# Wavelet mixing on one core: eight equal rounds of four pieces, batch innermost, first steps turned during the mixing

## The chip, the cores and the metric

One Trainium2 chip, one core in use. The metric is the device time of one execution in microseconds (us), the median over the runs of a kernel.

## The reference, cut to what matters

x is (8, 32, 512, 512) in float32: 8 batches of 32 channels, 256 images of 512 by 512. A wavelet transform of four levels is taken of every image, and only the coarsest coefficients (42 by 42 in each of four bands) are mixed between channels, by weights that differ from coefficient to coefficient; the rest passes through unchanged.

```python
yl, yh = _dwt2(x, _LEVEL)
yl_out = jnp.einsum('bixy,ioxy->boxy', yl, w_yl)
yh_out = yh[:-1] + [jnp.einsum('bicxy,iocxy->bocxy', yh[-1], w_yh)]
return _idwt2(yl_out, yh_out)
```

Since synthesis undoes analysis, the kernel computes out = x + synthesis(mixed coefficients - coefficients). The four bands of an image together are an 84 by 84 block of coefficients; the weights are 84 * 84 * 32 * 32 numbers, 28.9 MB, and each is used for the eight batches only.

## The kernel before, in words

The kernel has three phases, each written out per engine with its own semaphores; no planner sets the order. One image is 1 MB in float32.

**Analysis** (`turn1`, lines 373, 524 and 660): 32 turns of eight images. SP loads them into the eight slots of `x_sb`; PE reduces each along the height (`h_stage`, L333), ACT copies (L507), PE goes on along the width (L346, L357, L365) and the coefficients of 32 channels collect in `coef`. Once in a batch `channels_stage` (L378) turns them so that the channel and the row within a group of four lie on the partitions, and ACT's `copy_m` (L520) puts the result into `mix_sb`. The 84 rows are 21 groups ("lines") of four rows; four lines make a step, so that there are five full steps (FULL = 5) and a sixth with the one left-over line.

**Mixing** (`mix`, line 413): each full step is cut into six pieces of U = 14 columns (PARTS = 6), 30 pieces of 4 lines; the left-over line is another six pieces of one line each, at the end. For a piece, DVE (`build_low`, L680, three copies) and ACT (`build_high`, L553, one copy) lay the coefficients out block by block in one of two `diag` buffers; PE subtracts the old value (L420) and multiplies with the weights (L425, 56 matmuls, each recorded as two); ACT's `copy_mixed` (L560) copies the sum back to `mix_sb`. The weights come through a ring of three buffers (WBUFS = 3): SP waits for the piece that used a buffer (`weights_used`, L262) and loads 917,504 bytes (L258), or a quarter of that for a left-over piece. Two PSUM banks take turns. PE's loop `Fori(0, FULL)` has six pieces in its body; the left-over pieces are code of their own.

SP also loads six images of the next turn early (`load_early`, L265) into `work`: two ahead of the mixing, three among the pieces of the first step once the last channels are turned, one ahead of the left-over pieces.

**Synthesis** (`turn2`, lines 473 and 609): batches run backwards, the last one first. For each batch, `stage` takes its part of `mix_sb` (ACT's `copy_stage`, L585; for the first batch to be done DVE's L696, after all mixing), PE turns it back (`coefs_stage`, L449, four transposes a step), ACT's `copy_delta` (L593) stores it in `delta`. For each image ACT picks its block (L601), PE spreads it (`spread_stage`, L459), ACT copies (L607), PE finishes (`out_stage`, L469), DVE adds to the image (L703), SP stores it (L296), and POOL refills the slot (`refill`, L228) when the store has landed.

Within `mix_sb` an element is addressed as step, batch, line, column, so that the column is innermost:

```python
mix_sb = sb("mix_sb", [P, STEPS, BATCH, 4, ROWS])
```

Of the kernel before, what the change touches and what calls it, by code (L numbers as in the profile page):

```python
# [40 lines left out]
STEPS = -(-LINES // 4)  # L41
FULL = LINES // 4
U = 14
PARTS = ROWS // U
WBUFS = 3
QB = Q * BATCH
W_CHUNK = U * 4 * CHANNELS

# [76 lines left out]
def lines(v):  # L125
    return 4 if v < FULL else LINES - 4 * FULL


def wavelet_mix_kernel(nc, x, w_full, w_rest, consts, out):
# [3 lines left out]
    with ExitStack() as ctx:  # L133
# [6 lines left out]
        def sems(name, n):  # L140
# [6 lines left out]
        mix_sb = sb("mix_sb", [P, STEPS, BATCH, 4, ROWS])  # L147
        pick = sb("pick", [P, 2, ROWS])
        spread = sb("spread", [P, 2, SIZE])


        IMAGE = ROW_RUN * SIZE
        work = sb("work", [P, EARLY * IMAGE])
        along_h = work[:, 0:GROUP * SIZE].rearrange("p (m w) -> p m w", m=GROUP)
        at = GROUP * SIZE
# [3 lines left out]
        at += GROUP * ROWS  # L159
        coef = work[:, at:at + CHANNELS * ROWS].rearrange("p (r i) -> p r i", i=CHANNELS)  # L160
        used = at + CHANNELS * ROWS
        free = (EARLY * IMAGE - used) // IMAGE
        early = work[:, :].rearrange("p (a r w) -> p a r w", a=EARLY, r=ROW_RUN)
        early = [early[:, (e - free) % EARLY] for e in range(EARLY)]


        both = sb("both", [P, WBUFS * W_CHUNK + 2 * 4 * U * QB])
        w_sb = both[:, 0:WBUFS * W_CHUNK].rearrange("p (a n) -> p a n", a=WBUFS)
        at = WBUFS * W_CHUNK
        diag = both[:, at:at + 2 * 4 * U * QB].rearrange(  # L170
            "p (a l u n) -> p a l u n", a=2, l=4, u=U)
        delta = both[:, 0:2 * CHANNELS * ROWS].rearrange("p (a r) -> p a r", r=ROWS)
        assert 2 * CHANNELS * ROWS <= at
        stage = both[:, at:at + STEPS * Q * ROWS].rearrange("p (v r) -> p v r", v=STEPS)

# [4 lines left out]


# [16 lines left out]
        w_loaded = sems("w_loaded", WBUFS)  # L198
# [3 lines left out]
        mixed_copied = sems("mixed_copied", 2)  # L202
# [16 lines left out]
        def _(pool):  # L219
            nc.gpsimd.memset(mix_sb[:, FULL], 0.0).then_inc(cleared, 1)  # L220
# [22 lines left out]
        def _(sp):  # L243
# [12 lines left out]
            def load_w(c, v, weights):  # L256

                sp.dma_start(w_sb[:, c % WBUFS, 0:weights.shape[-1]], weights).then_inc(w_loaded[c % WBUFS], 16)  # L258

            def weights_used(c, v):  # L260

                sp.wait_ge(mixed[c % 2], PARTS // 2 * v + c // 2 + 2)  # L262
# [4 lines left out]
            for c in range(WBUFS):  # L267
                load_w(c, 0, w_full[c])
            for e in range(free):
                load_early(e)  # L270
            for c in range(WBUFS, PARTS):
                weights_used(c - WBUFS, 0)
                load_w(c, 0, w_full[c])
                sp.wait_ge(m_done, STEPS * BATCH)
                load_early(free + c - WBUFS)
            with sp.Fori(1, FULL) as v:
                for c in range(PARTS):
                    if c < WBUFS:
                        weights_used(c + PARTS - WBUFS, v - 1)
                    else:  # L280
                        weights_used(c - WBUFS, v)
                    load_w(c, v, w_full[PARTS * v + c])
            for e in range(free + WBUFS, EARLY):
                load_early(e)
            for c in range(PARTS):
                if c < WBUFS:
                    weights_used(c + PARTS - WBUFS, FULL - 1)
                else:
                    weights_used(c - WBUFS, FULL)
                load_w(c, FULL, w_rest[c])  # L290
# [24 lines left out]
        def _(pe):  # L315
            for a in range(2):
                pe.sem_inc(mixed[a], 1)
                pe.sem_inc(o_done[a], 1)
            pe.wait_ge(const_loaded, 16)
# [48 lines left out]
            def channels_stage(v, b):  # L368

                if v == 0:
                    pe.wait_ge(c_copied, CHANNELS // GROUP * (b + 1))
                if v >= 2:
                    pe.wait_ge(m_copied, STEPS * b + v - 1)
                for n in range(lines(v)):
                    h = Q * (4 * v + n)
                    last = nc.tensor.matmul(ps[:, 6 + v % 2, P * n:P * n + ROWS],  # L378
                                            coef[0:ROWS, h:h + Q].rearrange("p q i -> p (q i)"),
                                            const[0:ROWS, EYE:EYE + ROWS], start=True, stop=True, is_transpose=True)  # L380
                last.then_inc(m_done, 1)
# [25 lines left out]
            last_stage(HALVES * TURNS - 1)  # L407
            for v in range(STEPS):
                channels_stage(v, BATCH - 1)


            def mix(c, v, n):

                a, wb = c % 2, c % WBUFS
                w = w_sb[:, wb, 0:U * n * CHANNELS].rearrange("p (u l o) -> p u l o", u=U, l=n)
                pe.wait_ge(low_built[a], PARTS // 2 * v + c // 2 + 1)
                pe.wait_ge(high_built[a], PARTS // 2 * v + c // 2 + 1)
                pe.wait_ge(mixed_copied[a], PARTS // 2 * v + c // 2 + 1)
                for l in range(n):
                    nc.tensor.matmul(ps[32 * l:32 * l + 32, a, 0:U * QB], const[:, NEG:NEG + CHANNELS],  # L420
                                     diag[:, a, l].rearrange("p u n -> p (u n)"), start=True, stop=False)
                pe.wait_ge(w_loaded[wb], 16 * (PARTS // WBUFS * v + c // WBUFS + 1))
                for u in range(U):
                    for l in range(n):
                        last = nc.tensor.matmul(ps[32 * l:32 * l + 32, a, QB * u:QB * u + QB],  # L425
                                                w[:, u, l], diag[:, a, l, u], start=False, stop=u == U - 1)
                last.then_inc(mixed[a], 1)

            with pe.Fori(0, FULL) as v:
                for c in range(PARTS):  # L430
                    mix(c, v, 4)
            for c in range(PARTS):
                mix(c, FULL, lines(FULL))
            for a in range(2):
                pe.wait_ge(mixed_copied[a], STEPS * PARTS // 2 + 1)


            def coefs_stage(v, k, first=False):
# [3 lines left out]
                if first:  # L442
                    pe.wait_ge(first_staged, v + 1)
                else:
                    pe.wait_ge(staged, STEPS * (k - 1) + v + 1)
                if v >= 2:
                    pe.wait_ge(d_copied, STEPS * k + v - 1)
# [36 lines left out]
            for v in range(STEPS):  # L484
                coefs_stage(v, 0, first=True)
# [11 lines left out]
        def _(act):  # L497
            for a in range(2):
                act.sem_inc(mixed_copied[a], 1)
# [17 lines left out]
            def copy_m(v, b):  # L517
                n = lines(v)
                act.wait_ge(m_done, STEPS * b + v + 1)
                nc.scalar.copy(mix_sb[:, v, b, 0:n],  # L520
                               ps[:, 6 + v % 2, 0:P * n].rearrange("p (l r) -> p l r", l=n)[:, :, 0:ROWS],
# [20 lines left out]
            for v in range(STEPS):  # L542
                copy_m(v, BATCH - 1)


            def build_high(c, v, n):

                a = c % 2
                act.wait_ge(mixed[a], PARTS // 2 * v + c // 2 + 1)
                for q in range(Q - 1, Q):  # L550
                    part = slice(32 * q, 32 * q + 32)
                    src = mix_sb[part, v, :, 0:n, U * c:U * c + U].rearrange("p b l u -> p l u b")
                    last = nc.scalar.copy(diag[part, a, 0:n, :, BATCH * q:BATCH * (q + 1)], src)  # L553
                last.then_inc(high_built[a], 1)

            def copy_mixed(c, v, n):

                a = c % 2
                act.wait_ge(mixed[a], PARTS // 2 * v + c // 2 + 2)
                nc.scalar.copy(mix_sb[0:32 * n, v, :, :, U * c:U * c + U],  # L560
                               ps[0:32 * n, a, 0:U * QB].rearrange("p (u q b) -> p b q u", q=Q, b=BATCH),
                               ).then_inc(mixed_copied[a], 1)

            act.wait_ge(diag_cleared, 1)
            act.wait_ge(m_copied, STEPS * BATCH)
            build_high(0, 0, 4)
            build_high(1, 0, 4)
            with act.Fori(0, FULL - 1) as v:
                for c in range(PARTS):
                    copy_mixed(c, v, 4)  # L570
                    build_high((c + 2) % PARTS, v + (c + 2) // PARTS, 4)
            for c in range(PARTS):
                copy_mixed(c, FULL - 1, 4)
                after = FULL - 1 + (c + 2) // PARTS
                build_high((c + 2) % PARTS, after, lines(after))
# [166 lines left out]
```

## Time and profile before

| what | value |
|---|---|
| median of 3 runs | 2043.56 us (2043.24 to 2045.97) |
| the profiled execution's own time | 2043.87 us |
| its span in the profile | 2042.1 us |
| mean granted TensorE clock | 0.985 |
| analysis, up to the last matmul along the width | about 675 us |
| mixing, first to last matmul | 680.3 to 783.6 us |
| first `spread` matmul of the synthesis | 789.3 us |
| HBM traffic | 827 MB, mean 405 GB/s |

The profile's page shows one execution. Its parts give the busy time of each engine, forty slices of the span, the DMA queues, the chain of waits that ended last, and groups of instructions. PE is the matmul row and PEld the weight loads; SPq and POOLq are the queues' own DMA issues. "issue" is time in which an engine waited for nothing that the profile shows. Times in a timeline count from the start of the span.

### The profile page before, as it was taken

To read this page: it belongs to the slowest core of one execution; us is meant where nothing else is said; L and a number is where in the kernel's file an instruction comes from. 1 tells how busy PE (TensorE), PEld (TensorE's weight loads), DVE (VectorE), ACT (ScalarE), POOL (GpSimd) and SP (SyncE) were. 2 spreads that over 40 slices of the span, in tenths; PEclk is the share of its full clock that TensorE was granted. 3 is DMA by queue.
4 is the path that set the end of the run, shared out by engine and by line. 5 is a ranking of instruction groups with operands and counts; after the bars stand their busy time and mean duration, and the time that the engine had idled before them with its cause. 6 is when DMAs were issued, how large, how long until landed. Compare 5 with 4: busy or idle time off the path is not lost.

```text
span 2042.1 us, 44418 instructions
## 1 busy us (share of the span) xinstructions
PE 1882.5 (92%) x17580; PEld 943.2 (46%) x17580; DVE 827.2 (41%) x947; ACT 460.0 (23%) x1043; POOL 131.7 (6%) x249
## 2 busy tenths in 40 slices
PE   6999999999999778999999999999999999999996
PEld 3656666666666444444443343343333333334332
DVE  1222222222222354555544444444444444444443
ACT  1222222222222353121121121121121121112110
POOL 0000000000000000011111111111111111111110
PEclk8899999999999799999999999999999999999998
DMA  8999999999999695999999999999999999999998
GB/s 352 365 374 411 422 422 422 422 422 422 422 422 421 262 338 207 387 412 427 427 428 427 427 427 428 427 428 427 428 427 428 427 428 427 428 427 426 422 424 336
DMA packets 114794, 827.16 MB, mean 405 GB/s; under 512 B 12752, under 2 KB 13520, under 8 KB 17488
## 3 DMA queue, kind: packets, MB, share of 16 engines
q1 hardware_dynamic: 79920, 573.01, 67.8%
q0 software_dynamic: 34848, 253.77, 29.7%
q8 instruction: 21, 0.34, 0.1%
q14 instruction: 5, 0.04, 0.0%
HBM read 558.29 MB, written 268.44 MB: 405 GB/s over the span
## 4 chain that ended last, share of the span: by engine, by line
DMA 48%; PE 13%; issue 3%; DVE 2%; DVEq 0%; ACT 0%; POOLq 0%; SPq 0%
DMA out<-x_sb 32%; DMA x_sb<-x 14%; PE ps L469 8%; PE ps L459 2%; DMA both<-w_full 2%; DVE x_sb L703 2%; PE ps L425 1%; PE ps L420 1%; DMA both<-w_rest 0%; PE ps L449 0%; DVEq L715 0%; DVEq L133 0%; POOLq L228 0%; SPq L296 0%; ACT both L593 0%
## 5 line engine op out<-in xcount | busy, mean ns | idle before, releaser
L469 PE MATMUL ps<-spread,const 128*128 128x512 f32 x2048 | 940.0, 602 | 72.5 <-DVE x_sb L703 72.4
L703 DVE TENSOR_TENSOR x_sb<-ps,x_sb 128x1024 f32<-128x1024 f32 x500 | 592.7, 1220 | 626.1 <-DMA x_sb<-x 540.1
L469 PEld LDWEIGHTS ps<-spread,const 128*128 128x128 f32 x2048 | 373.5, 190 | 636.5 <-issue 407.8
L607 ACT COPY spread<-ps 84x512 f32<-84x512 f32 x256 | 148.8, 581 | 928.4 <-PE ps L459 928.0
L333 PE MATMUL ps<-x_sb,const 32*32 32x512 f32 x8192 | 293.9, 608 | 37.6 <-DMA x_sb<-x 31.6
L346 PEld LDWEIGHTS ps<-const,work 128*128 128x128 f32 x2048 | 252.0, 196 | 56.9 <-ACT work L507 42.3
L346 PE MATMUL ps<-const,work 128*128 128x84 f32 x2048 | 260.8, 281 | 3.4 <-ACT work L507 3.4
L459 PE MATMUL ps<-const,pick 128*84 128x512 f32 x512 | 261.3, 592 | 0.7 <-issue 0.7
L228 POOL DMA_DIRECT2D x_sb<-x x242 | 128.1, 529 | 1885.0 <-DMA out<-x_sb 1885.0
L507 ACT COPY work<-ps 128x512 f32<-128x512 f32 x256 | 131.4, 600 | 421.8 <-PE ps L333 421.8
L333 PEld LDWEIGHTS ps<-x_sb,const 32*32 32x32 f32 x8192 | 139.3, 104 | 141.5 <-issue 102.0
L652 DVE COPY work<-ps 128x336 f32<-128x336 f32 x256 | 129.9, 507 | 181.5 <-PE ps L346 181.5
L658 DVE COPY work<-ps 128x336 f32<-128x336 f32 x64 | 32.5, 507 | 325.9 <-PE ps L357 325.9
L459 PEld LDWEIGHTS ps<-const,pick 128*84 128x84 f32 x512 | 77.3, 153 | 121.5 <-issue 121.5
L680 DVE COPY both<-mix_sb 32x448 f32 (+1 forms) x108 | 52.9, 489 | 53.7 <-PE ps L425 50.0
L601 ACT COPY pick<-both 84x84 f32 (+1 forms) x256 | 66.8, 261 | 9.3 <-issue 9.3
L425 PE MATMUL ps<-both 128*32 128x32 f32 x3528 | 46.0, 206 | 24.7 <-DMA both<-w_full 12.7
L425 PEld LDWEIGHTS ps<-both 128*32 128x32 f32 x3528 | 43.8, 118 | 52.4 <-DMA both<-w_full 29.5
L357 PE MATMUL ps<-work,const 128*32 128x336 f32 x512 | 50.6, 468 | 0.6 <-DVE work L652 0.6
L365 PE MATMUL ps<-work,const 128*84 128x336 f32 x128 | 48.0, 458 | 0.6 <-DVE work L658 0.6
L420 PE MATMUL ps<-both,const 128*32 128x448 f32 x252 | 38.9, 623 | 2.8 <-ACT both L553 1.6
L593 ACT COPY both<-ps 84x512 f32 (+3 forms) x48 | 23.0, 529 | 65.5 <-PE ps L449 65.5
(23 smaller groups left out, 246.6 us busy)
## 6 DMA issues: line engine op xcount, KB each, us to landing
x_sb<-x SPq DMA_DIRECT2D x256, 1024.0 KB, 9.9
out<-x_sb SPq DMA_DIRECT2D x250, 1024.0 KB, 25.2
x_sb<-x POOLq DMA_DIRECT2D x242, 1024.0 KB, 11.0
both<-w_full SPq DMA_DIRECT2D x30, 896.0 KB, 6.7
work<-x SPq DMA_DIRECT2D x6, 1024.0 KB, 9.1
out<-work SPq DMA_DIRECT2D x6, 1024.0 KB, 10.1
both<-w_rest SPq DMA_DIRECT2D x6, 224.0 KB, 3.4
const<-consts SPq DMA_DIRECT2D x1, 888.0 KB, 4.5
```

Source lines behind the costliest of these rows:

```text
L228: pool.dma_start(x_sb[:, c], x_rows[first + c]).then_inc(x_reloaded[c], 16)
L333: last = nc.tensor.matmul(ps[to:to + TILE, m], const[part, A3H + TILE * r:A3H + TILE * r + TILE], x_sb[part, GROUP * a + m, r], start=r == ...
L346: last = nc.tensor.matmul(ps[:, 4 + m % 2, ROWS * k:ROWS * k + ROWS], along_h[:, m, P * k:P * k + P], const[:, A4 + ROWS * m:A4 + ROWS * ( ...
L420: nc.tensor.matmul(ps[32 * l:32 * l + 32, a, 0:U * QB], const[:, NEG:NEG + CHANNELS], diag[:, a, l].rearrange("p u n -> p (u n)"), start=T ...
L425: last = nc.tensor.matmul(ps[32 * l:32 * l + 32, a, QB * u:QB * u + QB], w[:, u, l], diag[:, a, l, u], start=False, stop=u == U - 1)
L459: nc.tensor.matmul(ps[0:ROWS, p], pick[:, p], const[:, SW:SW + SIZE], start=True, stop=True).then_inc(s_done[p], 1)
L469: last = nc.tensor.matmul(ps[:, 2 + k], const[:, SH + P * k:SH + P * k + P], spread[:, p], start=True, stop=True)
L507: nc.scalar.copy(along_h[:, m], ps[:, m]).then_inc(h_copied, 1)
L601: nc.scalar.copy(pick[0:ROWS, p], delta[0:ROWS, o]).then_inc(picked[p], 1)
L607: nc.scalar.copy(spread[0:ROWS, p], ps[0:ROWS, p]).then_inc(s_copied[p], 1)
L652: nc.vector.tensor_copy(turned[:, :, m], ps[:, 4 + m % 2, 0:SEGS * ROWS].rearrange("p (k r) -> p k r", k=SEGS),).then_inc(t_copied, 1)
L703: nc.vector.tensor_tensor(part, ps[:, 2 + 2 * half:4 + 2 * half], part, ALU.add).then_inc(added[half], 1)
```

## The change

- The left-over line is mixed first, in two pieces: its 84 columns are laid out as 4 times 14 and 4 times 7 columns in the places of the four lines. With the 30 full pieces that makes 32, run as eight rounds of four (PE `Fori(0, ROUNDS)`); the second piece's unused half is multiplied by zeros. Step 0 is now the one-line step.
- The weights have four buffers and the mixing four PSUM banks. All memory of mixing lies in `work`, apart from one early image that has a place of its own. SP loads four pieces and that image up front, two images when the last turn and the last coefficients are done, and the last three when the last four pieces are mixed.
- `mix_sb` has the batch innermost. `build_low` and `build_high` read runs of eight numbers, `copy_mixed` writes such runs, `copy_m` writes and `copy_stage` reads every eighth number.
- The last batch's channels are turned into six different PSUM banks, with no wait for copies between them; building of the first two pieces starts when step 0 is copied.
- In every round, between its second and third piece, PE makes the four transposes of `first_coefs`: those of a finished step in rounds 1, 2, 4, 5, 7 and after the last, and of no use in the other rounds. ACT's `copy_first` and `copy_delta` take the place of L696 and of the six turns after mixing.
- ACT's and DVE's mixing code is no longer a loop.

```diff
-        mix_sb = sb("mix_sb", [P, STEPS, BATCH, 4, ROWS])
+        mix_sb = sb("mix_sb", [P, STEPS, 4, ROWS, BATCH])
...
+LEFT = (U, U // 2)
+PIECES = len(LEFT) + PARTS * FULL
+RING = 4
+ROUNDS = PIECES // RING
+TURNED = {1: 0, 2: 1, 4: 2, 5: 3, 7: 4, 8: 5}
...
+            for k in range(RING):
+                load_w(k)
+            load_early(2)
+            sp.wait_ge(t_done, TURNS * SLOTS)
+            load_early(0)
+            sp.wait_ge(c_done, TURNS * HALVES)
+            load_early(1)
+            for k in range(RING, PIECES):
+                piece_mixed(k - RING)
+                load_w(k)
+            for e in range(3, EARLY):
+                piece_mixed(PIECES - RING + e - 3)
+                piece_mixed(PIECES - RING + e - 2)
                 load_early(e)
...
+            def mix(j, i):
+                a = j % 2
+                w = w_sb[:, j].rearrange("p (u l o) -> p u l o", u=U, l=4)
+                pe.wait_ge(low_built[a], RING // 2 * i + j // 2 + 1)
+                pe.wait_ge(high_built[a], RING // 2 * i + j // 2 + 1)
+                pe.wait_ge(mixed_copied, RING * i + j + 1)
+                if j >= 2:
+                    pe.wait_ge(m_copied, STEPS * BATCH)
...
+            def first_coefs(i):
+                pe.wait_ge(first_staged, i + 1)
+                pe.wait_ge(d_copied, i + 1)
+                for q in range(Q):
+                    last = nc.tensor.matmul(ps[0:ROWS, 6, P * q:P * q + P], first_stage[:, ROWS * q:ROWS * (q + 1)],
+                                            const[:, EYE:EYE + P], start=True, stop=True, is_transpose=True)
+                last.then_inc(d_done, 1)
+
+            with pe.Fori(0, ROUNDS) as i:
+                mix(0, i)
+                mix(1, i)
+                first_coefs(i)
+                mix(2, i)
+                mix(3, i)
+            first_coefs(ROUNDS)
...
-            for v in range(STEPS):
-                coefs_stage(v, 0, first=True)
...
+            for k in range(PIECES):
+                if k % RING == 0 and k // RING not in TURNED:
+                    act.sem_inc(first_staged, 1)
+                if k + 2 < PIECES:
+                    build_high(k + 2)
+                copy_mixed(k)
+                i, j = divmod(k, RING)
+                if j == 2:
+                    if i in TURNED:
+                        copy_delta(TURNED[i], 0, i + 1)
+                    else:
+                        act.wait_ge(d_done, i + 1)
+                        act.sem_inc(d_copied, 1)
+                for at, v in TURNED.items():
+                    if k == last_piece(v):
+                        copy_first(v, at)
...
-            for a in range(2):
-                dve.wait_ge(mixed_copied[a], STEPS * PARTS // 2 + 1)
-            for v in range(STEPS):
-                nc.vector.tensor_copy(stage[:, v], mix_sb[:, v, BATCH - 1].rearrange("p q r -> p (q r)"),
-                                      ).then_inc(first_staged, 1)
```

## Rows read from the trace of the kernel before

**Rows 1.** The page: span, 40 slices of DMA and GB/s, the synthesis's adds
```profile
span 2042.1 us, 44418 instructions
...
DMA  8999999999999695999999999999999999999998
GB/s 352 365 374 411 422 422 422 422 422 422 422 422 421 262 338 207 387 412 427 427 428 427 427 427 428 427 428 427 428 427 428 427 428 427 428 427 426 422 424 336
...
L703 DVE TENSOR_TENSOR x_sb<-ps,x_sb 128x1024 f32<-128x1024 f32 x500 | 592.7, 1220 | 626.1 <-DMA x_sb<-x 540.1
```

**Rows 2.** Windows: busy PE, PEld, DVE, ACT, POOL; PE clock, DMA share, GB/s
```profile
675.00:680.00 5.00, 2.71 (x23) 1.81 (x21) 2.73 (x6) 3.33 (x8) 0.00 (x0) 1.00 0.00 0
...
695.00:700.00 5.00, 2.99 (x118) 1.87 (x112) 1.59 (x3) 1.49 (x2) 0.00 (x0) 0.50 0.96 344
...
700.00:705.00 5.00, 2.20 (x99) 1.33 (x93) 0.86 (x3) 0.85 (x2) 0.00 (x0) 0.84 0.62 243
...
780.00:785.00 5.00, 3.85 (x74) 2.69 (x72) 1.45 (x6) 1.97 (x4) 0.00 (x0) 1.00 0.10 35
785.00:790.00 5.00, 3.70 (x26) 2.30 (x24) 0.84 (x4) 3.30 (x8) 0.00 (x0) 1.00 0.00 0
```

**Rows 3.** Waits from 670 to 800: us in total, times, longest
```profile
PE ps L425 <- DMA both<-w_full: 12.7, 15, 2.0
...
PE ps L425 <- issue: 10.7, 5, 4.3
```

**Rows 4.** Timeline of PE and of the DVE's first build, start and length in us
```profile
677.19 3.29 DVE L680 COPY both<-mix_sb 32x448 f32 x6 [2.61 <-ACT mix_sb L520]
...
680.27 1.72 PE L420 MATMUL ps<-both,const 128*32 128x448 f32 x8 [1.60 <-ACT both L553]
...
709.70 1.60 PE L425 MATMUL ps<-both 128*32 128x32 f32 x112
...
711.90 1.16 PE L425 MATMUL ps<-both 128*32 128x32 f32 x112
...
713.93 1.15 PE L425 MATMUL ps<-both 128*32 128x32 f32 x112
...
739.98 0.96 PE L420 MATMUL ps<-both,const 128*32 128x448 f32 x8 [0.32 <-issue]
...
771.27 1.16 PE L425 MATMUL ps<-both 128*32 128x32 f32 x112 [0.38 <-DMA both<-w_full]
```

**Rows 5.** DMA: 652 to 672, then 720 to 765; packets, MB, share; us to landing
```profile
q1 hardware_dynamic: 1204, 8.41, 101.4%
...
q1 hardware_dynamic: 2410, 15.33, 94.9%
...
both<-w_full SPq DMA_DIRECT2D x17, 896.0 KB, 6.7
```

**Rows 6.** The chain that ended last, from 766 on: start, length in us
```profile
766.59 7.72 DMA both<-w_rest
...
783.65 0.54 ACT mix_sb L560
...
785.41 0.59 ACT both L593
786.01 0.14 issue
786.14 0.62 PE ps L449 x4
...
789.30 1.92 PE ps L459 x4
```

**Rows 7.** Groups by form (first two: 664 to 800; last: from 800), mean ns
```profile
L553 ACT COPY both<-mix_sb 32x448 f32 x24 | 22.8, 950 | 0.6
L560 ACT COPY mix_sb<-ps 128x448 f32 x24 | 13.1, 544 | 39.8 <-PE ps L425 39.8
...
L585 ACT COPY both<-mix_sb 128x336 f32 x42 | 17.7, 471 | 0.0
```

More of the change, by code:

```diff
@@ L158, in wavelet_mix_kernel @@
         third = work[:, at:at + GROUP * ROWS]
[L159 to L168, printed above, removed]
@@ new lines, in wavelet_mix_kernel @@
+        w_sb = work[:, AT_W:AT_DIAG].rearrange("p (a n) -> p a n", a=RING)
+        diag = work[:, AT_DIAG:AT_DIAG + 2 * 4 * U * QB].rearrange("p (a l u n) -> p a l u n", a=2, l=4, u=U)
+        assert AT_DIAG + 2 * 4 * U * QB <= AT_EARLY
+        early = [0, IMAGE, AT_EARLY] + [AT_W + IMAGE * e for e in range(EARLY - 3)]
+        early = [work[:, e:e + IMAGE].rearrange("p (r w) -> p r w", r=ROW_RUN) for e in early]
+        APART = -(-(AT_W + IMAGE * (EARLY - 3) - 2 * IMAGE) // ROWS)
+        at = 2 * IMAGE + (APART + CHANNELS) * ROWS
@@ L316, in _ @@
             for a in range(2):
-                pe.sem_inc(mixed[a], 1)
                 pe.sem_inc(o_done[a], 1)
+            pe.sem_inc(d_copied, 1)
+            for c in range(RING):
+                pe.sem_inc(mixed_copied, 1)
             pe.wait_ge(const_loaded, 16)
@@ L408, in _ @@
             for v in range(STEPS):
[L409 to L420, printed above, removed]
+                channels_stage(v, BATCH - 1, LAST_BANKS[v])
@@ new lines, in mix @@
+            def mix(j, i):
[6 more added lines that the diff above has]
+                    pe.wait_ge(m_copied, STEPS * BATCH)
+                for l in range(4):
+                    nc.tensor.matmul(ps[32 * l:32 * l + 32, j, 0:U * QB], const[:, NEG:NEG + CHANNELS],
@@ L541, in _ @@
             copy_c(HALVES * TURNS - 1)
-            for v in range(STEPS):
[L543 to L554, printed above, removed]
@@ L567, in _, with build_high @@
[L567 to L575, printed above, removed]
-            for c in range(PARTS):
-                copy_mixed(c, FULL, lines(FULL))
-                if c + 2 < PARTS:
-                    build_high(c + 2, FULL, lines(FULL))
+            def build_high(k):
+                a, part = k % 2, slice(32 * (Q - 1), 32 * Q)
+                if k >= 2:
+                    act.wait_ge(mixed[a], k // 2)
+                nc.scalar.copy(diag_of(k)[part, :, :, BATCH * (Q - 1):BATCH * Q], lines_of(k)[part]).then_inc(high_built[a], 1)
@@ new lines, in copy_mixed, with copy_first @@
+            def copy_mixed(k):
+                act.wait_ge(mixed[k % 2], k // 2 + 1)
+                for to, of in sums_of(k):
+                    last = nc.scalar.copy(to, of)
+                last.then_inc(mixed_copied, 1)
+            def copy_first(v, i):
+                act.wait_ge(mixed_copied, RING + last_piece(v) + 1)
+                act.wait_ge(d_done, i)
+                nc.scalar.copy(first_stage[:].rearrange("p (q r) -> p q r", q=Q), mix_sb[:, v, :, :, BATCH - 1],
+                               ).then_inc(first_staged, 1)
@@ new lines, in copy_delta @@
+            def copy_delta(v, k, done):
+                n, h = lines(v), first_row(v)
+                bank = (6 + v % 2) if done is None else 6
+                act.wait_ge(d_done, STEPS * k + v + 1 + IDLE if done is None else done)
+                to = delta[0:ROWS, bass.ds(APART * (k & 1), CHANNELS), h:h + Q * n]
+                of = ps[0:ROWS, bank].rearrange("p (q l o) -> p o l q", q=Q, l=4)[:, :, 0:n]
+                nc.scalar.copy(to.rearrange("p o (l q) -> p o l q", q=Q), of).then_inc(d_copied, 1)
@@ L626, in turn2 @@
                         copy_stage(2 * c + 1, batch)
-            for v in range(STEPS):
-                copy_delta(v, 0)
-            act.wait_ge(d_copied, STEPS)
+            copy_delta(FULL, 0, ROUNDS + 1)
+            act.wait_ge(d_copied, STEPS + IDLE + 1)
             pick_image(0, 0)
```

203 lines of the change are left out of this document (99 added, 104 removed).

## The prediction

> **What bounds the kernel now.** I read the page's slices first. From the second slice on, the DMA engines are full, but in slices 13 to 16 (about 660 to 820 us) the rate falls from 422 to 262, 338, 207 and 387 GB/s [rows 1]. The synthesis runs at 427 GB/s, and DVE's adds there waited 540.1 us for images [rows 1]: the DMA is its bound, so an earlier first store should come out as an earlier end, one for one. The analysis is DMA-bound at 422 GB/s too, and the change leaves its loads alone. So the question is how much shorter the stretch without full traffic becomes, measured at the first `spread` matmul, now at 789.30 us [rows 6].
>
> The windows show three holes: from 675 to 680 nothing moves, from 700 to 705 the share is 0.62, and from 780 to 790 it is 0.10 and then 0.00 [rows 2]. The waits name what holds PE within the mixing: 10.7 us in five waits for "issue", in the middle of runs of L425 where no semaphore is waited for (I read these as PE waiting for its own code, on the first pass through the loop), and 12.7 us for weights [rows 3]. The timeline gives the pace: from the seventh piece's L425 (709.70) to the thirtieth's (771.27) are 23 pieces, 61.57 us, 2.68 us a piece [rows 4]. Pieces whose weights were there follow each other at 2.03 to 2.20 us (713.93 - 711.90 and 711.90 - 709.70) [rows 4]. A weight load takes 6.7 us from issue to landing [rows 5]; with three buffers that, the 1.16 us of L425 and some 0.2 us of semaphores make 8.06 us for three pieces, 2.69 us each. This agrees with the pace: the ring's latency sets it, not PE and not the DMA's full rate. That the DMA could do more is in the queue's rows: 8.41 MB in 20 us around 660, when weights were queued behind images, but 15.33 MB in 45 us (341 GB/s) in the mixing, at a share of 94.9% [rows 5]. I take the 94.9% as packets that lie half waiting, since the earlier window moved more at about the same share.
>
> **The change, part by part.**
>
> **Start.** PE's first L420 starts at 680.27, after DVE's six copies from 677.19 on and both `build_high` copies [rows 4]. Now only step 0, one line, need be copied before building; three copies take half of 3.29 us, 1.65 us. From some 676.8 on that gives a first matmul at 678.4: 1.9 us gained. PE has 21 transposes without waits meanwhile. The copies of step 0's piece back to `mix_sb` are four on ACT in place of one (4 * 0.54 = 2.2 us), but four PSUM banks are free before anyone needs them: nothing.
>
> **First round.** From 680.27 to 708.2 (L425 at 709.70 less its 1.5 us of L420) six pieces took 28 us, 4.7 us each, code waits and half clock included [rows 4]; the granted clock there was 0.50 to 0.84 [rows 2]. Four pieces cost 18.7 us by that, and four transposes 0.62 + 0.14 us [rows 6]: 19.5 us. Between bounds (all 10.7 * 4/6 = 7.1 us of code waits gone, or as before) I take 18 us: only weights are loaded beside the code now, while before an image came with each of three pieces; two images instead use the empty stretch from 675 on. End of round 0: 696.4.
>
> **Rounds 1 to 7.** PE needs 4 * 2.1 us, 0.76 us for the transposes and the 0.32 us that the loop's turn shows [rows 4]: 9.5 us. The DMA needs 4 * 0.9175 MB at 420 GB/s, 8.7 us. The ring of four gives a load 9.5 - 1.16 - 0.2 = 8.1 us to land, against 6.7 measured at a lighter rate. So PE sets the round: 7 * 9.5 = 66.5 us. PE was at half clock after the waits of the first pass (L425 1.60 us at 709.70, 1.16 later [rows 4]); I add 1.5 us for one or two such pieces. End of mixing: 764.4, against 783.65 [rows 6]. This includes the left-over line, which cost 17 us at the end before (766.59 to 783.65, 7.72 of it a wait behind an early image [rows 6]), and is now two pieces of 32.
>
> The transposes bring PE waits for `first_staged` and `d_copied`, with `mix` 2 and 3 queued behind them. In rounds 2 and 5 the step they need ended with the round before, so ACT has two pieces (4.2 us) for `copy_mixed`, `copy_first` and a build, together 0.54 + 0.5 to 0.8 + 0.95 us [rows 7]: hidden, with 2 us left. ACT waits for `d_done` ahead of `copy_first` in rounds 3 and 6, some 0.7 us, and builds a piece later by that; PE has a built piece in hand. Per piece ACT has 1.5 us of work and DVE 1.65 us [rows 4, 7], under the 2.1: nothing. Contiguous runs of eight should make the builds faster, at most by the 0.4 us between L553 and L560 [rows 7]; off the path.
>
> **Tail.** Before, 5.65 us lie between the last mixing matmul and `spread` (783.65 to 789.30 [rows 6]). Now it is one step: `copy_mixed` 0.54, `copy_first` 0.6, transposes 0.62, `copy_delta` 0.59, pick 0.26, five handovers of 0.1 or less: 3.2 us, if the code behind the loop is there. First spread at 767.6, 21.7 us earlier. SP's queue: the last three early images are issued as pieces 29 to 32 end, ahead of the first store. 3.1 MB at 422 GB/s are 7.5 us, and from the last piece's end to the first store lie some 3.2 + 6.8 us (before, 789.3 to 796.1). They fit in that hole.
>
> **Batch innermost.** ACT's `copy_stage` (42 times in the synthesis, 471 ns [rows 7]) now reads with a step of 32 bytes. The nearest row of a strided read is L553: 950 ns for 448 elements a partition, against 544 for L560 from PSUM [rows 7], 0.9 ns an element more. For 336 elements that is +0.3 us, 12.8 us in all, between nothing and that; and likewise for `copy_m`'s writes in the analysis, 35 full copies, at most 10.6 us. Both lie on ACT, beside a full DMA with loads in flight, so I cost them at nothing; without the cover at most 23 us would show. The Trainium skill ("SBUF — State Buffer", the note on cachelines) says that each access that leaves a 16-byte line pays, which takes in a step of eight fp32 numbers: by it the upper ends hold, and the sum would move only if ACT lay on the path. L680 on DVE, 0.55 us each with the same stride as L553 [rows 4], shows no such price on that engine.
>
> **Sum.** The steps are one chain of times, 678.4 + 18 + 66.5 + 1.5 + 3.2 = 767.6, and 789.3 - 767.6 = 21.7 us. 2043.87 (the profiled execution) - 21.7 = 2022.2 us; the median is 0.3 us lower, so **2022 us**.
>
> **The rivals.**
>
> **A. The DMA keeps its pace of 2.68 us a piece**, since its share was 94.9% already [rows 5]. For: that share. Against: 8.41 MB in 20 us. A round is then 10.7 us, 7 of them 8.5 us more: 2030.5 us. Chance 0.20.
>
> **B. The synthesis gives part back.** The three images at the end delay the first stores and refills, and strided copies hold up `spread` at seven batch boundaries: up to 7.5 us of images, up to 1 us a boundary. 2022 + 7 = 2029 to 2036 us. Against: the hole of 10 us, and ACT's idle share there. Chance 0.12.
>
> **C. The loop's code is fetched in every round.** Its waits took 10.7 us for six pieces [rows 3], 7.1 us for four; seven more rounds of that cost 50 us, so 2072 us, slower than before. It decides from 3.1 us a round on (21.7 / 7). For: the loop has transposes and four full pieces of code in it. Against: the old loop had six pieces, and its second pass shows 0.32 us at the turn and no wait inside a run [rows 4]. Chance 0.04. The Trainium skill ("Runtime: NRT & Kernel Launch", Instruction fetch mechanics) says that a taken branch whose target is outside a window of two pages forces a fetch, though it gives PE a larger memory than the others; by the two pages alone C would hold, and the old loop's second pass speaks against that.
>
> **D. Half clock through the mixing**: 3.2 us a piece (1.72 + 1.49, about the first one's) in place of 2.1 makes 31 us more, 2053 us. The clock fell when PE stood idle [rows 2], and there is less of that now. Chance 0.02.
>
> **How the numbers follow.** My forecast has 0.62. Its own range: code waits gone (-7), pieces at 2.03 us (-2), tail and start as said, 2013; up to the first round at 19.5 us and one code wait of 4.3 us behind the loop, 2028. With A and B the range is 2013 to 2034 us. A measurement of this kernel tells some 0.2%, 4 us, from no change. Faster by more than that: 0.93; within 0.2%: 0.02 (several costs of B in full, on top of A); slower: 0.05 (C, most of D).
>
> **What would show it.** Right: in the profile after, the first `spread` matmul near 768 us; 28 pieces after round 0 at 2.4 us each; the slices of GB/s without the 207; no copy of L696; PE's waits for weights under 5 us in all; synthesis of the same length as before, 1252.8 us from first spread to end (2042.1 - 789.3). Wrong: 10 us or more a round with PE waiting for weights (A); a synthesis over 1256 us (B); "issue" waits inside L425 runs after the first round (C); L425 runs of 1.5 us or more beyond 705 (D).

## The result and the profile after

The changed kernel takes 2006.43 us (median of 6 runs, 2001.11 to 2009.59) against 2040.74 us for the kernel before (6 runs, 2034.57 to 2045.97): a ratio of 0.983, with a 95% interval of 0.9809 to 0.9851. The gain is 1.7%, and the interval lies clear of 1. The forecast was faster, 2022 us with a range of 2013 to 2034; the measured time lies below the range. Two later pairs of the same kernels gave 0.9862 (0.9836 to 0.9888) and 0.9848 (0.9823 to 0.9873), so the gain is 27 to 34 us, where 21.7 were forecast. The three runs that I started from (median 2043.56 us) lie high among the runs of the kernel before: 23 later ones have a median of 2036.39 us.

The page of the changed kernel, profiled in its fastest run (2001.11 us; its span is 1999.5), shows the lines of [rows 1] again:

```profile
span 1999.5 us, 44393 instructions
...
PEclk9999999999999999999999999999999999999999
DMA  9999999999999898999999999999999999999997
GB/s 395 399 369 405 421 422 422 421 422 422 422 422 422 335 400 361 373 427 427 427 427 427 427 427 427 427 427 427 427 427 427 427 427 427 428 424 417 424 426 335
...
q8 instruction: 18, 0.29, 0.1%
...
L757 DVE TENSOR_TENSOR x_sb<-ps,x_sb 128x1024 f32<-128x1024 f32 x500 | 592.7, 1220 | 630.0 <-DMA x_sb<-x 543.0
```

The hole of four slices has become a dent: 335, 400, 361, 373 in place of 262, 338, 207, 387 GB/s. (A slice of the kernel before is 51 us, so its four run from 664 to 868 us; the prediction gave 820 us as their end, which changes nothing in its sum.) The adds of the synthesis wait for images as long as before (543.0 against 540.1 us), so the synthesis is still bound by the DMA.

The chain of waits of the changed kernel shows the new order (start, length in us). In this kernel L468 subtracts the old value, L473 multiplies with the weights, L482 transposes, L614 is `copy_first` and L512 the first `spread`:

```profile
669.79 0.96 PE ps L468 x8
...
672.94 0.95 issue
...
676.55 1.35 issue
...
680.20 1.18 issue
...
682.59 0.96 PE ps L468 x8
...
691.21 0.96 PE ps L468 x8
692.17 0.96 PE ps L473 x70
693.12 0.91 PE ps L468 x8
694.03 0.96 PE ps L473 x70
694.99 0.57 PE ps L482 x4
695.55 0.89 PE ps L468 x8
...
699.37 0.42 issue
699.79 0.96 PE ps L468 x8
...
742.83 0.54 ACT mix_sb L607
743.39 0.80 ACT const L614
744.24 0.64 PE ps L482 x4
744.87 1.01 issue
745.88 1.92 PE ps L512 x4
```

Round 0 runs from 669.79 to 682.59 (12.8 us) with three waits for issue, 3.5 us in all, against five and 10.7 us before [rows 3]. Then a round takes 8.58 us (691.21 to 699.79): four pieces of 1.90 us in the mean, 0.57 us of transposes, 0.42 us for the turn of the loop (the branch back to its start). The rounds that begin at 716.99 and 725.65 take 8.66 and 8.79 us. The tail from 742.83 to 745.88 is one step's copies and transposes, 3.05 us.

**Where the difference between the two profiles lies.** Executions differ in their analysis, so I count from the start of the last matmul along the width (L357 before, L400 after) to the first `spread` matmul. Before: 673.6 to 789.3, and 669.0 to 781.5 in a second trace, 115.7 and 112.5 us. After: 665.3 to 745.9, 670.3 to 752.7 and 665.1 to 745.7, that is 80.6, 82.4 and 80.6 us. The mean falls by 32.9 us (114.1 to 81.2). The synthesis, from the first `spread` to the end, took 1252.8 and 1253.0 us before and 1253.6, 1255.0 and 1255.1 us after: 1.7 us are given back there. The profiled pair differs by 42.6 us: 35.1 in this stretch and 8.3 because its analyses ended that far apart, less 0.8 in the synthesis.

### The profile page after: what moved, and what is told of

Read it like the earlier page. It is cut to its first block, busy times and chain, and to the rows that moved or that the text cites. A ratio compares the mean times of both kernels' runs of the same rounds, so it can differ in the third digit from the quotient of the medians.

```text
span 1999.5 us, 44393 instructions
## 1 busy us (share of the span) xinstructions
PE 1859.7 (93%) x17652; PEld 931.5 (47%) x17652; DVE 810.1 (41%) x930; ACT 480.8 (24%) x1047; POOL 132.2 (7%) x249
## 4 chain that ended last, share of the span: by engine, by line
DMA 58%; PE 33%; issue 4%; DVE 2%; SPq 1%; ACT 0%; DVEq 0%; POOLq 0%; ACTq 0%
DMA out<-x_sb 32%; DMA x_sb<-x 26%; PE ps L376 11%; PE ps L522 8%; PE ps L389 6%; PE ps L512 2%; DVE x_sb L757 2%; PE ps L473 2%; PE ps L468 1%; PE ps L400 1%; SPq L300 1%; PE ps L408 1%; PE ps L423 1%; ACT mix_sb L572 0%; PE ps L482 0%
## 5 line engine op out<-in xcount | busy, mean ns | idle before, releaser
L757 DVE TENSOR_TENSOR x_sb<-ps,x_sb 128x1024 f32<-128x1024 f32 x500 | 592.7, 1220 | 630.0 <-DMA x_sb<-x 543.0
L389 PEld LDWEIGHTS ps<-const,work 128*128 128x128 f32 x2048 | 246.5, 193 | 54.6 <-ACT work L557 40.2
L512 PE MATMUL ps<-const,pick 128*84 128x512 f32 x512 | 261.3, 592 | 1.0 <-issue 1.0
L389 PE MATMUL ps<-const,work 128*128 128x84 f32 x2048 | 255.4, 277 | 2.0 <-ACT work L557 2.0
L512 PEld LDWEIGHTS ps<-const,pick 128*84 128x84 f32 x512 | 77.3, 153 | 121.9 <-issue 121.9
L663 ACT COPY pick<-work 84x84 f32 (+1 forms) x256 | 66.7, 261 | 9.8 <-issue 9.6
L400 PE MATMUL ps<-work,const 128*32 128x336 f32 x512 | 50.5, 463 | 1.6 <-issue 1.0
L742 DVE COPY work<-mix_sb 32x448 f32<-32x448 f32 (+1 forms) x96 | 36.4, 380 | 36.9 <-PE ps L473 31.7
L473 PEld LDWEIGHTS ps<-work 128*32 128x32 f32 x3584 | 36.9, 109 | 20.4 <-issue 10.0
L473 PE MATMUL ps<-work 128*32 128x32 f32 x3584 | 37.5, 198 | 3.5 <-issue 3.5
L623 ACT COPY work<-ps 84x512 f32 (+3 forms) x48 | 24.0, 529 | 55.8 <-PE ps L502 54.5
L563 ACT COPY work<-ps 84x336 f32 (+1 forms) x64 | 27.8, 435 | 39.3 <-PE ps L408 39.3
```

The lines of the kernel that those rows point to most:

```text
L389: last = nc.tensor.matmul(ps[:, 4 + m % 2, ROWS * k:ROWS * k + ROWS], along_h[:, m, P * k:P * k + P], const[:, A4 + ROWS * m:A4 + ROWS * ( ...
L400: last = nc.tensor.matmul(ps[TILE * k:TILE * k + TILE, 6, 0:GROUP * ROWS], const[:, at:at + TILE], turned[:, k].rearrange("p m r -> p (m r ...
L473: last = nc.tensor.matmul(ps[32 * l:32 * l + 32, j, QB * u:QB * u + QB], w[:, u, l], diag[:, a, l, u], start=False, stop=u == U - 1)
L512: nc.tensor.matmul(ps[0:ROWS, p], pick[:, p], const[:, SW:SW + SIZE], start=True, stop=True).then_inc(s_done[p], 1)
L757: nc.vector.tensor_tensor(part, ps[:, 2 + 2 * half:4 + 2 * half], part, ALU.add).then_inc(added[half], 1)
```

## The experiments

Each starts from the changed kernel unless it says otherwise. "Rounds 1 to 7" is from the first L468 of round 1 to the start of the last L473; 60.0 us in the first profile (682.59 to 742.6), 61.6 in the second (687.85 to 749.4).

### Three and two weight buffers in use

```diff
-            for k in range(RING):
+            for k in range(3):
                 load_w(k)
...
-            for k in range(RING, PIECES):
-                piece_mixed(k - RING)
+            for k in range(3, PIECES):
+                piece_mixed(k - 3)
```

> The changed kernel, but SP loads the weights of piece k only when piece k-3 is mixed, so that only three of the four buffers are ever in use; the four PSUM banks stay. Theory (the fourth weight buffer sets the pace of the rounds): a load of some 7 us, 1.16 us of L473 and 0.2 us of semaphores per three pieces make 2.6 to 2.7 us a piece, rounds 1 to 7 grow from 60.2 us to 73 to 75 us, and the time from 2006 to about 2019 us. Rival (the round was short for other reasons, clock and faster builds): rounds of 8.6 to 9.0 us and a time within 3 us of the changed kernel.

With 2 in place of 3:

> The changed kernel, but SP loads the weights of piece k only when piece k-2 is mixed, so that two buffers are in use. Theory (a ring of n buffers gives a piece every (latency + 1.36 us) / n, until the DMA is full): the latency falls to 4.5 to 5.5 us with less in flight, so 3.0 to 3.4 us a piece, rounds 1 to 7 of 85 to 95 us, and about 2035 us. Rival (bytes set the pace): under 2.8 us a piece, under 2025 us.

Three: 2014.07 us (4 runs), ratio to before 0.9899 (0.986 to 0.9939). Two: 2031.82 us (10 runs), ratio 0.9967 (0.9949 to 0.9984). Rounds 1 to 7 take 70.7 us for three (685.27 to 756.0) and 82.3 us for two (693.99 to 776.3). The DMA view from 690 to 740 us has the latencies; first the changed kernel:

```profile
q1 hardware_dynamic: 3236, 20.62, 101.3%
...
work<-w_full SPq DMA_DIRECT2D x21, 896.0 KB, 7.3
```

Three buffers in use:

```profile
q1 hardware_dynamic: 2813, 17.90, 97.7%
...
work<-w_full SPq DMA_DIRECT2D x20, 896.0 KB, 6.5
```

Two:

```profile
q1 hardware_dynamic: 2379, 15.13, 87.3%
...
work<-w_full SPq DMA_DIRECT2D x17, 896.0 KB, 4.7
```

The last column is the median time to landing. With the 1.36 us of L473 and handovers, (4.7 + 1.36) / 2, (6.5 + 1.36) / 3 and (7.3 + 1.36) / 4 give 3.03, 2.62 and 2.17 us a piece; measured over 28 pieces are 2.94, 2.53 and 2.14. That the sums agree does not say what limits: with all buffers kept in use they must agree, since the latency of each is taken from the same run. What shows the cause is that the pace changed when the number of buffers alone did. So up to three buffers the ring's depth sets the pace, as the theory said; with four the latency has grown to 7.3 us and the DMA is at its full rate (20.62 MB in 50 us, 412 GB/s, at a share of 101.3%). A share of 97.7% still left 13% of the bytes on the table: the share is no proof of a full DMA. The fourth buffer is worth 70.7 - 60.0 = 10.7 us in the rounds here, a third of the 32.9 us. The expected ranges (73 to 75 us for three, 85 to 95 for two) began 2 to 3 us too high, and the times came out lower than expected too (2014.07 for 2019 us, 2031.82 for 2035 us).

### No transposes in the rounds

```diff
-TURNED = {1: 0, 2: 1, 4: 2, 5: 3, 7: 4, 8: 5}
+TURNED = {3: 0, 4: 1, 5: 2, 6: 3, 7: 4, 8: 5}
...
-                first_coefs(i)
                 mix(2, i)
                 mix(3, i)
-            first_coefs(ROUNDS)
+            for i in TURNED:
+                first_coefs(i)
```

with the three useless turns counted ahead, and ACT's copies after the last piece.

> The changed kernel with no transposes in the rounds; the six steps of the first batch are copied, turned and copied one after another when all is mixed, with a single stage buffer. Theory (rounds are at the DMA's full rate, 3.67 MB at 420 GB/s are 8.7 us): taking 0.6 us of PE out of each round leaves it at 8.5 to 8.7 us; the tail grows from 3.05 us to 6 * 2.1 = 12 to 13 us, and the time by 8 to 10 us. Rival (PE sets the round): rounds of 8.0 us, 4 us back in the rounds, and the time grows by 5 us only.

2018.94 us (4 runs), ratio 0.9915 (0.9883 to 0.9948): 10 to 14 us above the changed kernel's medians, where 8 to 10 were expected. Rounds 1 to 7 take 59.9 us (682.36 to 742.3), the same as with transposes: the theory holds. PE's weight loads wait for weights for 15.7 us now (second line), against 9.6 (changed kernel, first line):

```profile
PEld ps L473 <- DMA work<-w_full: 9.6, 22, 0.8
```

```profile
PEld ps L475 <- DMA work<-w_full: 15.7, 23, 0.8
```

So what the transposes took is waited for, and in the rounds PE (8.6 us with them) and the DMA (3.67 MB a round, 8.76 us at the 419 GB/s of its windows) are balanced within 2%: the changed kernel's rounds begin at PE's pace (8.58 and 8.60 us) and end at the DMA's (8.79). The tail grew from 3.1 to 14.7 us (742.3 to 757.0), 11.6 us where 9 to 10 were expected: PE fell to half clock in it, and four transposes took 1.09 us in place of 0.65. The windows show the clock (0.50) and the empty DMA (columns as in [rows 2]):

```profile
750.00:755.00 5.00, 2.25 (x9) 1.31 (x10) 0.00 (x0) 2.55 (x4) 0.00 (x0) 0.50 0.00 0
755.00:760.00 5.00, 3.99 (x8) 1.68 (x9) 0.00 (x0) 1.68 (x5) 0.00 (x0) 0.50 0.01 2
```

### PE's rounds written out

```diff
-            with pe.Fori(0, ROUNDS) as i:
+            for i in range(ROUNDS):
```

> The changed kernel with PE's eight rounds written out instead of a loop. Theory (the waits for issue inside runs of L473 in round 0 are PE waiting for its code, which the loop needs once): they appear in every round, some 3.5 us a round, in all 25 us, and more where the DMA is full; the time grows by 20 to 50 us. Rival (they are something else of the start, such as the clock or semaphores): waits in round 0 only, the time within 3 us, or 3 us less for the turn of the loop.

2052.49 us (6 runs), ratio 1.0077 (1.0052 to 1.0103): slower than the kernel before. Rounds 1 to 7 take 106.0 us. The page's instruction queue (packets, MB), the waits from 670 to 765 (us, times, longest) and PE's timeline of this kernel:

```profile
q8 instruction: 45, 0.74, 0.1%
```

```profile
PE ps L473 <- issue: 31.9, 21, 2.4
```

```profile
707.14 0.40 PE L473 MATMUL ps<-work 128*32 128x32 f32 x24 [1.85 <-issue]
...
711.17 0.38 PE L473 MATMUL ps<-work 128*32 128x32 f32 x21 [1.41 <-issue]
...
714.83 0.32 PE L473 MATMUL ps<-work 128*32 128x32 f32 x14 [1.56 <-issue]
...
719.20 0.27 PE L473 MATMUL ps<-work 128*32 128x32 f32 x7 [2.36 <-issue]
```

The instruction queue moved 45 packets of 16 KB in place of 18, 27 more for 28 more pieces of code, and there is one wait a piece in the rows above, each a little further on in the run of L473 (24, 21, 14 and 7 matmuls left). That is PE waiting for the next block of code. The waits in round 0 are the same thing, and the loop pays it once. The theory's price of 3.5 us a round was too low, though the total of 46 us lies in its range of 20 to 50: a written-out round costs 6.6 us more than one of the loop. The waits are 1.5 us each in the mean (31.9 in 21), 6.1 us for the four pieces of a round; in the first pass of the loop there were three waits, 3.5 us in all. PE also fell to half clock for some pieces (a granted clock of 0.66 from 720 to 730 us).

### The two images among the pieces of round 0

```diff
-            load_early(0)
             sp.wait_ge(c_done, TURNS * HALVES)
-            load_early(1)
             for k in range(RING, PIECES):
                 piece_mixed(k - RING)
                 load_w(k)
+                if k < RING + 2:
+                    load_early(k - RING)
```

> The changed kernel with the two images that it loads at the end of the analysis loaded behind the weights of the fifth and sixth piece instead, as the kernel before did. Theory (round 0 was shorter than forecast since PE's code came through an emptier DMA): the waits for issue in round 0 grow from 3.5 us to 6 to 9 us, PE falls to half clock for some pieces, round 0 grows from 12.8 to 16 to 20 us and the time by 3 to 7 us. Rival (the code comes at the same speed whatever the DMA carries): round 0 within 1 us, and only the 2 MB are paid later, up to 5 us where the rounds are DMA-bound, seen as weight waits in rounds 1 and 2.

2008.97 us (4 runs), ratio 0.9865 (0.9839 to 0.989), beside 2009.23 us and 0.9862 for the changed kernel run beside it: the 3 to 7 us that the theory gave do not show in the time. The trace has the effect on round 0 that it gave: the stretch from the last L400 (667.5) to the first `spread` (753.1) is 85.6 us, 4.4 more than the mean of 81.2. Round 0 took 16.6 us (671.98 to 688.62), with code waits of 0.41, 3.82 and 2.07 us, 6.3 in all, and the half clock behind them (L468 1.72 us instead of 0.96):

```profile
682.00 1.13 PE L473 MATMUL ps<-work 128*32 128x32 f32 x74 [3.82 <-issue]
682.98 1.72 PE L468 MATMUL ps<-work,const 128*32 128x448 f32 x8
...
687.40 0.79 PE L473 MATMUL ps<-work 128*32 128x32 f32 x68 [2.07 <-issue]
```

So the code does come more slowly while images are being moved. From the last L400 to the end of the span this kernel took 1338.9 us (667.5 to 2006.4), the changed kernel 1334.2, 1337.4 and 1335.7 in its three traces: 3.1 us more than their mean. Medians of four runs that spread over 4 to 6 us don't separate that from nothing.

### The same two images after the mixing

```diff
             load_early(2)
-            sp.wait_ge(t_done, TURNS * SLOTS)
-            load_early(0)
-            sp.wait_ge(c_done, TURNS * HALVES)
-            load_early(1)
...
                 load_early(e)
+            for e in range(2):
+                load_early(e)
```

> The changed kernel with the two images that it loads at the end of the analysis loaded behind the three late ones instead, as pieces end and before the first stores. Theory (an emptier DMA brings PE's code sooner, and the stretch between the last piece and the first stores has room for 2 MB more, 5 us): the waits for issue in round 0 fall from 3.5 us to 0.5 to 2 us, the synthesis keeps its 1253 to 1255 us, and the kernel is 1 to 3 us faster than the changed one. Rival (that stretch is already used up by the three images): the first stores land later, the synthesis grows by 3 to 5 us, and the kernel is 1 to 3 us slower.

> The changed kernel once more, beside the one with both images late, for a time on the same chip. Both theories: from the last matmul along the width to the first spread matmul 80 to 83 us, and its median within 4 us of 2007 us.

2008.85 us (6 runs) against 2005.12 us (5 runs) for the changed kernel beside it, with ratios to before of 0.9864 and 0.9848 whose intervals overlap: no gain shown, and a loss of 1 to 3 us (the rival) not excluded. PE's waits for code in round 0 stayed as they were (us, times, longest; L471 is this kernel's L473):

```profile
PE ps L471 <- issue: 3.5, 3, 1.6
```

So moving these two images out of the analysis's end did not shorten them. They do depend on what else is being moved, though: in round 0 they come to 2.2 us with two weight buffers in use (0.95, 0.68 and 0.62), 3.2 us with three, 3.5 us with four and 6.3 us with the images among the pieces. (With two buffers PE also waited 0.5 us for weights there, during which code could come.) The synthesis did not grow either, 1254.9 us, so the stretch between the last piece and the first stores takes the 2 MB; but nothing is won by it: from the last width matmul (668.6) to the end (2004.2) are 1335.6 us, where the changed kernel has a mean of 1335.8. The changed kernel's third trace came out as expected (80.6 us, 2005.12 us).

### The old layout alone

```diff
-        mix_sb = sb("mix_sb", [P, STEPS, 4, ROWS, BATCH])
+        mix_sb = sb("mix_sb", [P, STEPS, BATCH, 4, ROWS])[:].rearrange("p s b l r -> p s l r b")
```

> The changed kernel with the column innermost in the mixed coefficients again, as before. Theory (the new layout moves costs off and on ACT and DVE without touching the path): the builds go back to about 540 ns on DVE and 950 ns on ACT, the copies into the mixed coefficients from 844 to about 440 ns, and those to the stage from some 830 to about 470 ns; three DVE builds take 1.65 us against a piece of 1.9 us, so a round stays at 8.6 to 8.8 us and the time within 3 us. Rival 1 (the builds were what held PE before): rounds of 9 us and more, 3 to 8 us slower. Rival 2 (the dear copies at the seven batch boundaries cost the analysis something): the analysis ends 1 to 4 us earlier and the kernel is faster by that.

2011.25 us (4 runs), ratio 0.9874 (0.9836 to 0.9911); rounds 1 to 7 take 60.2 us (686.60 to 746.8). The forms in the mixing of this kernel (busy us, mean ns):

```profile
L742 DVE COPY work<-mix_sb 32x448 f32<-32x448 f32 x93 | 50.2, 540 | 23.0 <-PE ps L473 20.0 <-ACT mix_sb L572 2.1
...
L601 ACT COPY work<-mix_sb 32x448 f32<-32x448 f32 x31 | 29.3, 945 | 3.8 <-PE ps L473 2.8
L607 ACT COPY mix_sb<-ps 128x448 f32<-128x448 f32 x30 | 28.5, 950 | 1.8 <-PE ps L473 1.1
```

and of the changed kernel, in the mixing, the analysis and the synthesis:

```profile
L742 DVE COPY work<-mix_sb 32x448 f32<-32x448 f32 x93 | 35.6, 383 | 36.8 <-PE ps L473 31.7 <-ACT mix_sb L572 4.3
...
L601 ACT COPY work<-mix_sb 32x448 f32<-32x448 f32 x31 | 17.4, 561 | 25.1 <-PE ps L473 24.9
```

```profile
L572 ACT COPY mix_sb<-ps 128x336 f32 x35 | 24.7, 785 | 3.6 <-PE ps L423 2.9
```

```profile
L654 ACT COPY work<-mix_sb 128x336 f32 x42 | 31.5, 800 | 0.0
```

The layout moves costs in both directions and the rounds don't notice. With the old one ACT was busy 9.54 us of the 10 from 700 to 710, against 5.74 with the new one, but the DMA set the pace in both. (`copy_mixed` costs 950 ns here and not the 544 of [rows 7]; this version goes through the batches innermost, where the kernel before wrote runs of columns, so it is the old layout but not the old copy.) The dear copies at the batch boundaries cost the analysis nothing that its spread would show (669.0 us at a clock of 0.95 in the first 200 us).

### Both kernels once more

> The kernel before, once more, for a second trace of it. The two profiled executions differ by 8.3 us already in the analysis, which the change hardly touches. Theory (the start of an execution varies from run to run with the clock that PE has in its first 200 us): this trace's analysis ends anywhere from 665 to 675 us, with a granted clock below 1 in the first 200 us in proportion, and its mixing lasts 110 us as before (first to last mixing matmul 103 us). Rival (the change shortens the analysis): 673 us again, within 1 us.

> The changed kernel once more. Theory: from the last matmul along the width to the first spread matmul 81 us within 1 us, from there to the end 1253 to 1254 us, and an analysis that varies between executions by some us with the clock in the first 200 us. Rival (the analysis is shorter by the change): 665 us again, within 1 us.

2037.89 us (12 runs) and 2009.23 us (4 runs). The analysis ends anywhere between 664.9 and 677.0 us over the twelve traces of all versions (start of the last matmul along the width), and the clock of the first 200 us goes with it. The window of those 200 us in the kernel before (673.6 us), in the one with two buffers (677.0 us) and in the changed kernel (665.3 us); the last three columns are clock, DMA share and GB/s:

```profile
0.00:200.00 200.00, 173.16 (x2859) 112.08 (x2859) 43.12 (x80) 42.87 (x86) 3.61 (x7) 0.93 0.92 374
```

```profile
0.00:200.00 200.00, 173.82 (x2763) 111.25 (x2764) 43.97 (x81) 44.48 (x86) 3.61 (x7) 0.91 0.91 367
```

```profile
0.00:200.00 200.00, 172.30 (x2965) 112.74 (x2976) 46.48 (x86) 50.80 (x97) 3.61 (x7) 0.98 0.96 392
```

The second trace of the kernel before has 0.96 and 669.0 us, that of the changed kernel 0.97 and 670.3. So the spread of executions is there in both kernels, as the theory said. That the clock is its cause is not shown: the DMA's rate in these windows falls with it, and either could come first. With two traces of the kernel before, a small effect of the change on the analysis is not excluded.

For the rest the expectations were a little off: the mixing of the kernel before, first to last matmul, took 99 us in this trace in place of 103, and the changed kernel's second trace has 82.4 us for the stretch and 1255.0 us for the synthesis, where 80 to 82 and 1253 to 1254 were expected.

## Why the prediction was wrong in its size

The order of things was right: the synthesis stayed DMA-bound and moved forward with the first `spread`, the holes were where it said, the tail came out at 3.05 us (3.2 forecast), and the start, from the last width matmul to the first mixing matmul, at 4.5 us where 6.7 less 1.9, 4.8, were forecast. Two terms were too large, and the base was too high.

- **First round: 18 us forecast, 12.8 measured** (13.1 in the second trace). I scaled the old first round to four pieces, half clock included, and took 1.5 us off for the lighter DMA. But the code waits are 3.5 us and not some 5.6 (7.1 less 1.5), and in the first profile PE never fell to half clock in it. The experiment with the images in round 0 brings back 3.8 us of this (16.6 us) by the two steps named; the rest I can only argue: the old round carried three images, not two, and began at half clock (L420 1.72 us [rows 4]). My low bound for it, with the 7.1 us gone, was 12.4 us, so the measured 12.8 lies inside it. (The range took 7 us off the 18, which gives 11 and counts 1.4 us twice.)
- **Rounds 1 to 7: 66.5 + 1.5 us forecast, 60.2 measured** (682.59 to 742.83). This is the step that failed. The 2.03 us between pieces whose weights seemed to be there [rows 4] were read as PE's own pace, and PE was given 2.1 us a piece, 8.4 a round; measured are 1.90 and 7.6, with 0.57 us of transposes for 0.76 and 0.42 us at the turn for 0.32, which together make 8.58 for 9.48. The half clock for which 1.5 us were added did not occur in the first profile; the second trace has it at the start of round 1 and takes 61.6 us. The old interval of 2.03 us had waits in it. The weight loads of that piece in the kernel before:

```profile
713.16 0.16 PEld L420 LDWEIGHTS ps<-both,const 128*32 128x32 f32 x8 [0.21 <-DVE both L680]
...
713.59 0.13 PEld L425 LDWEIGHTS ps<-both 128*32 128x32 f32 x4 [0.28 <-DMA both<-w_full]
```

The second trace of the kernel before has two pieces without such waits, 1.76 us apart:

```profile
704.88 1.16 PE L425 MATMUL ps<-both 128*32 128x32 f32 x112
...
706.64 1.16 PE L425 MATMUL ps<-both 128*32 128x32 f32 x112
```

That error lies in the forecast's lower bound too ("pieces at 2.03 us, -2"), which is one reason why the range stopped at 2013. With PE's true pace the DMA's 8.7 us a round, which I had worked out and set aside, is as high: 8.6 us were measured, with and without the transposes. So "PE sets the round" failed as well: PE and the DMA set it together.

Together these are 5.2 + 7.8 = 13.0 us, against a stretch that ended 13.4 us sooner than forecast (80.6 us instead of 767.6 - 673.6 = 94.0).

**How this makes up the miss of 15.6 us.** The forecast took 21.7 us off; the mean stretch fell by 32.9 us and the synthesis gave 1.7 back, 31.2 in all, so the forecast of the gain was 9.5 us short. The other part is the base: the three runs lay 7.2 us above the later median of 2036.39 us. That makes 16.7 us, 1.1 more than the miss, within the spread of the medians. So somewhat more than half of it are the two terms, and the rest the base. Against the kernel before as it ran beside the changed one (2040.74 us) the base was only 2.8 us high and the gain 12.6 us short; the split is no surer than that. From 2036.39 us the same sum would have given 2014.7 us with a range of 2006 to 2027, still 5 to 10 us above the changed kernel's medians (2005.12 to 2009.23), at the range's very edge.

**The signs.** The 207 GB/s and the copy of L696 are gone, and PE's matmuls show no wait for weights worth a row (its weight loads show 9.6 us). A piece after round 0 takes 2.14 us and not 2.4, and the first `spread` came at 745.9 us and not 768, of which 8.3 us are an analysis that ended sooner.

**Rival A** (the DMA keeps its pace) is refuted, and its mechanism measured: 97.7% of share at 358 GB/s with three buffers in use, 101.3% at 412 with four. **Rival B** held in kind, with 1.7 us in the mean instead of 7 (two traces before, three after), and its sign, over 1256 us, did not come. What the 1.7 us are stays open. Nothing points at the strided copies: the old layout, without them, has one of the longest syntheses (1257.8 us), though it began at half clock. More late images did not lengthen it: with five of them it took 1254.9 us. In some traces the first `spread` matmuls ran at half clock (1.12 us in place of 0.59 in the second trace of the changed kernel), but its third has 1255.1 us without that. **Rival C** did not occur, and the written-out loop shows what it would have cost: 106.0 us for the seven rounds, 46 us more. The Trainium skill ("Runtime: NRT & Kernel Launch", Instruction fetch mechanics) speaks of blocks of 16 KB fetched in sequence. The traces agree on the size (0.29 MB in 18 packets); the order of the blocks they don't show. That page also says that kernels prefer code written out to a branch where they can; for PE's loop here the traces show the opposite, 46 us. **Rival D** did not occur.

**The layout** was costed at nothing, which holds as far as the traces tell (rounds of 60.2 us with the old one, 60.0 with the new, and an analysis and a synthesis within the spread of the others). My upper ends for its copies were too low: 800 against 471 ns for `copy_stage` is +0.33 us where 0.3 was the bound, and 785 against 441 ns for `copy_m`. The Trainium skill ("SBUF — State Buffer", the note on cachelines) says that an access which crosses to a new 16-byte line pays; the traces agree for ACT in both directions, for reads and for writes of every eighth number. DVE's builds gained as well, 539 to 383 ns, so my reading that L680 shows no such price on DVE was wrong.

## What to carry to other kernels

Where a ring of buffers feeds an engine, ask what one buffer more or less would do before asking whether the engine or the DMA is full: here a DMA share of 95 to 98% still hid 13 to 17% of its rate. The interval between two pieces whose data was there is a bound of the engine only if nothing in it was late: look at the waits of the weight loads too, or take the engine's own busy time. And take the base from more than three runs, when an earlier stage that the change hardly touches varies by 12 us between traces.

## What the runs showed of the hardware

- PE's code in a loop of four pieces (some 960 matmul and load records, about four packets of 16 KB by the count of the written-out version) is waited for in the first pass only; written out, 28 more pieces cost 27 more packets and 46 us, though the DMA was not full (a share of 0.67 to 0.78 in windows of 10 us from 690 to 740).
- Loading two images among the pieces of round 0 instead of before it changes a PE wait for code from 1.35 to 3.82 us, and PE runs at half clock behind it.
- ACT writes 336 numbers from PSUM into SBUF in 441 ns in a run and in 785 to 844 ns at a step of 32 bytes.
